# Self-attention phase: output projection, norm and query projection on 13 flat tiles of 128 tokens instead of 16 batches of 100

## The chip, the cores and the metric

The kernel runs on one core of a Trainium2 chip. The metric is the device time of one execution in microseconds (us). Four engines compute: TensorE (PE; its weight loads are a row of their own, PEld), VectorE (DVE), ScalarE (ACT) and GpSimd (POOL). SyncE (SP) only issues transfers. Each engine works through its own list of instructions in order, and they wait for each other on semaphores.

## The reference

A decoder block on x (16 batches of 100 tokens, 512 features): causal self-attention, cross-attention on a context of 361 tokens per batch, and a mixture of experts, each followed by a layer norm. The part that matters here:

```python
x = _layernorm(x + attn(x, w_q, w_k, w_v, w_o))      # causal, 16 heads of 32
q = (x @ Wq + bq).reshape(b, s, 16, 128)             # cross-attention, first step
q = _rmsnorm(q, qn_w)                                # per token and head
k = _rmsnorm(ctx @ Wk + bk, kn_w); v = ctx @ Wv + bv # 4 heads, each shared by 4 of q
out = softmax(q k^T / sqrt(128)) v @ Wo
```

## The kernel before

There are three phases, one behind the other: self-attention (tiles `a_...`), cross-attention (`b_...`), experts (`c_...`). The change is in the first, `self_attention_phase`, and in how the second loads the queries.

The first phase walks over the batches, one body per batch, in a software pipeline written by hand. `over_batches` writes out batches 0 and 1, loops over pairs up to batch 13, and writes out batches 14, 15 and a body 16 that has only the "back" half. Body i does on PE, in this order:

- front half, batch i: scores (L252, 16 small matmuls), the first 3 of 12 matmuls for V;
- back half, batch i-1: four transposes of the normed rows x1 (L266);
- the other 9 matmuls for V;
- back half: the query projection, four products (n = 0 to 3) of 12 matmuls with 512 columns each (`product3`, L65, `a_Wqh`). I call one product with its norm and transposes a **unit**: it gives 100 tokens x 4 heads;
- the transposes of the softmax (L288), which wait for POOL (L540); the transposes of units 0 and 1 (L232); probabilities times V (L300); four matmuls of the next pair's q or k projection (L212); the transposes of units 2 and 3; the other twelve of L212; the output projection (L65, `a_woh`, 12 matmuls), which the residual and norm on DVE follow (L511 to L518).

Products are made from high and low halves (names in h and l), so that each needs three matmuls per 128 rows of the contraction. For a unit, DVE adds the bias (L472) and squares (L479), POOL takes the power -1/2 (L547, L549), DVE scales (L437). After the transposes ACT makes the high half (L336) and DVE the low half (L442) in `a_qo`, two slots, and SP stores it to `q_d` (L196). ACT waits until a slot's last store has landed before it writes the slot again.

At the start the weights w_v, w_o and the four parts of Wq go through `a_stage`, two slots of 1 MB. ACT casts the high half (`split_hi`, L322), DVE subtracts (`split_lo`, L393), and then SP may refill the slot.

The second phase loads 400 KB of queries per group of four heads (`load_q`), two slots, 64 loads.

Of the kernel before, what the change touches and what calls it, by code (L numbers as in the profile page):

```python
# [69 lines left out]
def self_attention_phase(nc, sem, x_nat, xT, w_q, w_k, w_v, w_o, Wq, bq, qn_w, kn_w, causal, ident, x1_d, q_d):  # L70
# [5 lines left out]
    with ExitStack() as ctx:  # L76
# [21 lines left out]
        xs = sb("a_xs", [S, D])  # L98
# [7 lines left out]
        oTh, oTl = sb("a_oTh", [P, DC, S], F32R), sb("a_oTl", [P, DC, S], F32R)  # L106
        x1_s = sb("a_x1", [S, D])
        stat = sb("a_stat", [S, 6])
        mv = sb("a_mv", [S, 2])
        rstd = sb("a_rstd", [S, 1])  # L110
        x1Th, x1Tl = sb("a_x1Th", [P, DC, S], F32R), sb("a_x1Tl", [P, DC, S], F32R)
        qn = sb("a_qn", [S, XKV, XG * XHD])
        junk = sb("a_junk", [S, XG * XHD])
        qss = sb("a_qss", [S, XH])
        qrs = sb("a_qrs", [S, XH])
        qo = sb("a_qo", [P, 2, 2, XG * S], F32R)
# [25 lines left out]
        def over_batches(eng, body):  # L142

            body(0, 0, 0)
            body(1, 1, 0)
            with eng.Fori(1, B // 2 - 1) as pair:
                body(2 * pair, 0, pair)
                body(2 * pair + 1, 1, pair)  # L150
            body(B - 2, 0, B // 2 - 1)
            body(B - 1, 1, B // 2 - 1)
            body(B, 0, B // 2)
# [7 lines left out]
        def _(sp):  # L161
# [9 lines left out]
            sp.dma_start(xs[:], x_nat[0]).then_inc(x_in, 16)  # L171
            sp.dma_start(stage[:, 1], pieces[1][0]).then_inc(w_raw[1], 16)
            sp.dma_start(bq_s[:], bq.partition_broadcast(S)).then_inc(bq_in, 16)
            def body(i, par, pair):
                is_int = isinstance(i, int)
                back, front = not (is_int and i == 0), not (is_int and i == B)
                if par == 0 and has_next(pair):

                    sp.wait_ge(xT_lo, pair + 1)
                    if not back:  # L180
                        sp.wait_ge(qs_done, 2)
                    sp.dma_start(xTr[:], xT[bass.ds(pair + 1, 1)].rearrange("a p c t -> p (a c) t")).then_inc(xT_in, 16)
                if not back:
# [3 lines left out]
                if back:  # L187
                    wait(sp, x1_rdy, i)
                    sp.dma_start(x1_d[bass.ds(i - 1, 1)].rearrange("a t d -> t (a d)"), x1_s[:]).then_inc(x1_out, 16)
                    if front:  # L190
                        wait(sp, ysum, i)
                        sp.dma_start(xs[:], x_nat[bass.ds(i, 1)].rearrange("a t d -> t (a d)")).then_inc(x_in, 16)
                    for n in range(4):
                        wait(sp, qT_lo, 4 * (i - 1) + n + 1)
                        dst = q_d[bass.ds(4 * (i - 1) + n, 1)].rearrange("a p h t -> p (a h) t")
                        sp.dma_start(dst, qo[:, n % 2].bitcast(F32)).then_inc(q_out[n % 2], 16)  # L196
            over_batches(sp, body)
            sp.wait_ge(x1_out, 16 * B)
            for slot in q_out:
                sp.wait_ge(slot, 16 * 2 * B)  # L200

        @block.tensor
        def _(pe):
# [20 lines left out]
            def transpose_q(i, n):  # L224

                pe.wait_ge(q_rdy, 4 * (i - 1) + n + 1)
                if n < 2:
                    pe.wait_ge(q_ev, 4 * (i - 1) + 3 + n)
                else:
                    pe.wait_ge(qT_lo, 4 * (i - 1) + n - 1)  # L230
                for h in range(XG):
                    mm = pe.transpose(bank[4 + n % 2][:, h * S:(h + 1) * S],  # L232
                                      qn[:, n, h * XHD:(h + 1) * XHD], ident_s[0:S, 0:S])
                mm.then_inc(qT_done, 1)

# [4 lines left out]
            def body(i, par, pair):  # L240
                is_int = isinstance(i, int)
                back, front = not (is_int and i == 0), not (is_int and i == B)
# [12 lines left out]
                if front:  # L255

                    pe.wait_ge(xT_lo, pair + 1)
                    if is_int and i == 0:
                        pe.wait_ge(w_lo, 1)
                    product3(pe, bank[7][0:S, :], lambda c: xTh[:, c, cols], lambda c: xTl[:, c, cols],  # L260
                             lambda c: wvh[:, c, :], lambda c: wvl[:, c, :], range(1), last=False)
                if back:

                    wait(pe, x1_rdy, i)
                    for c in range(DC):
                        mm = pe.transpose(bank[6][:, c * S:(c + 1) * S], x1_s[:, c * P:(c + 1) * P], ident_s[0:S, 0:S])  # L266
                    mm.then_inc(x1T_done, 1)
# [5 lines left out]
                if back:  # L273

                    wait(pe, x1T_lo, i)
                    for n in range(4):
# [1538 lines left out]
```

## Time and profile before

| | us |
|---|---|
| median of 3 runs | 1625.73 (1622.57 to 1629.63) |
| the profiled execution | 1628.02, of it the span 1626.2 |
| PE busy in the span | 1482.5 (91%) |
| DVE, ACT, POOL busy | 970.8, 655.5, 639.2 |
| mean granted clock of TensorE | 0.957 of 2.4 GHz |
| first phase | 0 to 529.2 |

Time is counted from the span's start. A timeline row has the start, the duration, engine, line, operation, names with shapes, and a count; in brackets the idle time ahead of it and what ended it. Durations of matmuls overlap, since they are pipelined: the pace is the distance from start to start.

### The profile page before, as it was taken

To read this page: it belongs to the slowest core of one execution; us is meant where nothing else is said; L and a number is where in the kernel's file an instruction comes from. 1 tells how busy PE (TensorE), PEld (TensorE's weight loads), DVE (VectorE), ACT (ScalarE), POOL (GpSimd) and SP (SyncE) were. 2 spreads that over 40 slices of the span, in tenths; PEclk is the share of its full clock that TensorE was granted. 3 is DMA by queue.
4 is the path that set the end of the run, shared out by engine and by line. 5 is a ranking of instruction groups with operands and counts; after the bars stand their busy time and mean duration, and the time that the engine had idled before them with its cause. 6 is when DMAs were issued, how large, how long until landed. Compare 5 with 4: busy or idle time off the path is not lost. (4 is left out here: it accounts for less than half of the span.)

```text
span 1626.2 us, 27742 instructions
## 1 busy us (share of the span) xinstructions
PE 1482.5 (91%) x8494; PEld 1217.7 (75%) x8494; DVE 970.8 (60%) x3587; ACT 655.5 (40%) x1762; POOL 639.2 (39%) x994
## 2 busy tenths in 40 slices
PE   7999999999995689999999999999999998479876
PEld 6778878778764478888888888888888887458754
DVE  3666566666664475556655566555665565744468
ACT  4443343344331254443444444344444444433344
POOL 1334333343342364444443444434344342262173
PEclk8999999999998789999999999999999999579988
DMA  6311212212212441112111111211112110756472
GB/s 204 107 67 62 100 60 78 86 58 81 81 51 86 150 132 42 60 54 64 56 45 59 54 59 39 67 59 54 53 42 68 53 43 21 293 139 167 138 223 81
DMA packets 60957, 139.75 MB, mean 86 GB/s; under 512 B 10182, under 2 KB 21034, under 8 KB 59876
## 3 DMA queue, kind: packets, MB, share of 16 engines
q1 hardware_dynamic: 56296, 123.85, 22.9%
q0 software_dynamic: 4576, 14.95, 3.7%
q8 instruction: 31, 0.51, 0.1%
q14 instruction: 54, 0.44, 0.1%
HBM read 94.31 MB, written 44.46 MB: 85 GB/s over the span
## 5 line engine op out<-in xcount | busy, mean ns | idle before, releaser
L913 ACT ACTIVATE b_probs<-b_probs,b_nmax 100x361 f32<-100x361 f32 x256 | 151.9, 593 | 70.7 <-DVE b_nmax L1011 70.4
L65 PE MATMUL b_bank<-b_kTh,b_q 128*100 128x362 f32 x512 | 174.3, 341 | 3.0 <-DVE b_kTl L993 1.7
L1123 POOL TENSOR_TENSOR b_pcarry<-b_half 128x1 f32<-128x1 f32 x176 | 41.7, 237 | 327.5 <-DVE b_rinv L1017 271.7
L1011 DVE CUSTOM_DVE_ANT_0 b_probs<-b_bank,b_mask 100x361 f32<-100x361 f32 x256 | 135.5, 529 | 56.9 <-issue 46.9
L1148 POOL TENSOR_SCALAR b_probs<-b_probs,b_rinv 100x361 f32<-100x361 f32 x256 | 157.4, 627 | 0.0
L1004 DVE TENSOR_TENSOR b_pTl<-b_bank,b_pTh 121x400 fp32r<-121x400 f32 x192 | 110.0, 573 | 52.6 <-ACT b_pTh L908 51.3
L908 ACT ACTIVATE b_pTh<-b_bank 121x400 fp32r<-121x400 f32 x192 | 96.8, 504 | 102.1 <-PE b_bank L754 99.9
L949 ACT ACTIVATE b_oTh<-b_bank,b_bv 128x400 fp32r<-128x400 f32 x64 | 38.1, 595 | 210.2 <-PE b_bank L65 210.2
L754 PE MATMUL b_bank<-b_ident,b_probs 100*121 100x100 f32 x768 | 110.4, 266 | 5.8 <-POOL b_probs L1148 5.8
L754 PEld LDWEIGHTS b_bank<-b_ident,b_probs 100*121 100x121 f32 x768 | 108.4, 187 | 8.2 <-POOL b_probs L1148 7.3
L65 PE MATMUL b_bank<-b_Woh,b_oTh 128*100 128x512 f32 x256 | 108.0, 422 | 1.4 <-DVE b_oTl L1078 1.4
L1078 DVE SCALAR_TENSOR_TENSOR b_oTl<-b_bank,b_bv,b_oTh 128x400 fp32r<-128x400 f32 x64 | 40.5, 633 | 109.0 <-ACT b_oTh L949 109.0
L65 PE MATMUL a_bank<-a_Wqh,a_x1Th 128*100 128x512 f32 x256 | 101.4, 396 | 2.6 <-DVE a_qn L472 1.4
L65 PEld LDWEIGHTS b_bank<-b_kTh,b_q 128*100 128x100 f32 x512 | 85.6, 167 | 22.0 <-issue 9.2
L65 PE MATMUL a_bank<-a_Wqh,a_x1Tl 128*100 128x512 f32 x256 | 101.7, 397 | 0.0
L65 PE MATMUL a_bank<-a_Wql,a_x1Th 128*100 128x512 f32 x256 | 101.4, 396 | 0.0
L65 PE MATMUL b_bank<-b_Woh,b_oTl 128*100 128x512 f32 x256 | 101.2, 395 | 0.0
L65 PE MATMUL b_bank<-b_Wol,b_oTh 128*100 128x512 f32 x256 | 101.2, 395 | 0.0
L65 PE MATMUL b_bank<-b_Wkh,b_ctxh 128*121 128x512 f32 x192 | 84.0, 437 | 16.2 <-DVE b_Wkl L966 16.2
L357 ACT ACTIVATE a_probs<-a_probs,a_nmax 100x100 f32<-100x100 f32 x256 | 92.8, 366 | 4.4 <-DVE a_nmax L425 4.4
L540 POOL TENSOR_TENSOR a_probs<-a_probs,a_rinv 100x400 f32<-100x400 f32 x64 | 54.6, 853 | 95.2 <-DVE a_rinv L432 95.1
L65 PE MATMUL b_bank<-b_kTl,b_q 128*100 128x362 f32 x256 | 84.8, 331 | 0.0
(241 smaller groups left out, 3981.1 us busy)
## 6 DMA issues: line engine op xcount, KB each, us to landing
q_d<-a_qo SPq DMA_DIRECT2D x64, 400.0 KB, 2.4
b_q<-q_d SPq DMA_DIRECT2D x64, 400.0 KB, 3.1
b_ctxr<-in_ctxT SPq DMA_DIRECT2D x48, 242.0 KB, 4.0
c_Eraw<-in_expert_w SPq DMA_DIRECT2D x16, 512.0 KB, 11.2
y_d<-c_y SPq DMA_DIRECT2D x32, 256.0 KB, 3.6
a_stage<-in_Wq SPq DMA_DIRECT2D x4, 1024.0 KB, 4.8
stage<-in_Wo SPq DMA_DIRECT2D x8, 512.0 KB, 3.7
a_xTr<-in_xT SPq DMA_DIRECT2D x8, 400.0 KB
```

The source lines that it names most:

```text
L65: mm = eng.matmul(out, lhsT=l(c), rhs=r(c), start=first and k == 0, stop=last and k == n - 1)
L357: e = act.activation(probs[:, r, c, :], probs[:, r, c, :], ACT.Exp, scale=-1.0, bias=nmax[:, h:h + 1], accum_out=psums[:, r, c:c + 1])
L540: pool.tensor_tensor(probs[:, r], probs[:, r], rinv[:, r].unsqueeze(2).to_broadcast([S, DC, S]), ALU.mult).then_inc(pn_rdy, 1)
L754: mm = pe.transpose(t_bank[c % 2][0:KT, h * S:(h + 1) * S], probs[:, s % 2, h, c * KT:(c + 1) * KT], ident_s[0:S, 0:S])
L908: act.activation(pTh[:, c, :], t_bank[c % 2][0:KT, 0:XG * S], ACT.Copy).then_inc(pt_hi, 1)
L913: act.activation(p, p, ACT.Exp, scale=-1.0, bias=nmax[:, s % 2, h:h + 1], accum_out=psums[:, s % 2, h:h + 1]).then_inc(e_rdy, 1)
L949: act.activation(oTh[:, kv, :], o_bank[:, 0:XG * S], ACT.Identity, bias=bv_s[:, kv:kv + 1]).then_inc(o_hi, 1)
L1004: dve.tensor_tensor(pTl[:, c, :], t_bank[c % 2][0:KT, 0:XG * S], pTh[:, c, :].bitcast(F32), ALU.subtract).then_inc(pt_lo, 1)
L1011: dve.tensor_tensor_reduce(out=probs[:, s % 2, h, 0:SE], in0=s_bank[h % 2][0:S, 0:SE], in1=mask_s[:], scale=-1.0, scalar=BIG, op0=ALU.add, ...
L1078: dve.scalar_tensor_tensor(out=oTl[:, kv, :], in0=o_bank[:, 0:XG * S], scalar=bv_s[:, kv:kv + 1], in1=oTh[:, kv, :].bitcast(F32), op0=ALU.add,
L1123: pool.tensor_tensor(pcarry[:, k:k + 1], half_s[:, 0:1], half_s[:, 0:1], ALU.add)
L1148: pool.tensor_scalar(p, p, rinv[:, s % 2, h:h + 1], 1.0, ALU.mult, ALU.mult).then_inc(p_rdy, 1)
```

## The change

The 1600 tokens of all batches are taken as one row of tokens and cut into tiles of 128: twelve full ones and one of 64. Output projection, residual, norm, x1 transposes and the units run per tile (52 units in place of 64; unit k is part k % 4 of tile k // 4). The attention output goes into a ring of two tiles (`a_oTh`, `a_oTl`), of which a batch writes 100 columns. Scores, softmax and V stay per batch. All loops are written out. `out_tile` says after which batch a tile is complete: none after batches 0, 4, 9 and 13, and the last after batch 15. `units` says how many units each of the 18 bodies takes. The weights go through the shared `stage` in halves of 512 KB, and w_o no longer has a slot from the start. `q_d` is laid out by tokens, so that one store writes 1024 pieces of 512 bytes, and one load reads 1024 pieces of 400 bytes.

```diff
-        pieces = [(w_v, wvh[:], wvl[:]), (w_o, woh[:], wol[:])]
-        pieces += [(Wq[n], Wqh[:, n], Wql[:, n]) for n in range(4)]
+        pieces = []
+        for w, h, l in [(w_v, wvh[:], wvl[:]), (w_o, woh[:], wol[:])] + [(Wq[n], Wqh[:, n], Wql[:, n]) for n in range(4)]:
+            pieces += [(w[:, c:c + 2], h[:, c:c + 2], l[:, c:c + 2]) for c in range(0, DC, 2)]
+        out_tile = {min((t * P + P - 1) // S, B - 1): t for t in range(NT - 1)}
+        units = [0, 0, 4, 3, 3, 2, 3, 4, 3, 3, 3, 3, 4, 3, 2, 4, 4, 4]
...
+            def store_q(k):
+                t, n = divmod(k, 4)
+                sp.wait_ge(qT_lo, k + 1)
+                sp.dma_start(q_d[n][:, :, :, tokens(t)], qo[:, k % 2, :, :, 0:rows(t)].bitcast(F32)).then_inc(q_out[k % 2], 16)
...
+            def queries(k, start):
+                t, n = divmod(k, 4)
+                pe.wait_ge(x1T_lo, t + 1)
+                if k - 2 >= start:
+                    pe.wait_ge(q_ev, k - 1)
+                else:
+                    wait(pe, qT_lo, k - 1)
...
+            def transpose_q(k, ks):
+                n = rows(k // 4)
+                pe.wait_ge(q_rdy, k + 1)
+                if k + 2 in ks:
+                    pe.wait_ge(q_ev, k + 3)
+                elif k - 2 in ks:
+                    pe.wait_ge(qT_lo, k - 1)
...
+                if i - 1 in out_tile:
+                    transpose_x1(out_tile[i - 1])
+                if i == B:
+                    pe.wait_ge(x1T_lo, NT - 1)
+                    output(NT - 1)
+                if i == B + 1:
+                    transpose_x1(NT - 1)
...
+                for k in ks:
+                    queries(k, ks[0])
...
+                for k in ks[:2]:
+                    transpose_q(k, ks)
...
+                for k in ks[2:]:
+                    transpose_q(k, ks)
...
+                if i in out_tile:
+                    output(out_tile[i])
...
-                src = q_d[bass.ds(n, 1)].rearrange("a p h t -> p (a h) t")
-                sp.dma_start(q_s[:, slot].bitcast(F32), src).then_inc(q_in[slot], 16)
+                src = q_d[n][:, :, :, bass.ds(j * S, S)]
+                sp.dma_start(q_s[:, slot].bitcast(F32).rearrange("p k (h t) -> p k h t", h=XG), src).then_inc(q_in[slot], 16)
...
-    q_d = nc.dram_tensor("q_d", (B * XKV, P, 2, XG * S), F32, kind="Internal").ap()
+    q_d = nc.dram_tensor("q_d", (XKV, P, 2, XG, B * S), F32, kind="Internal").ap()
```

**Place 1: ACT at the start of the program.** Before, the first casts of weights (`a_wvh`, `a_woh`, `a_Wqh`) and the exponentials of batches 0 and 1 (`a_probs`) stand so:

```order
L322 ACTIVATE a_wvh<-a_stage 128x2048
L322 ACTIVATE a_woh<-a_stage 128x2048
L357 ACTIVATE a_probs,a_psums<-a_probs,a_nmax 100x100 x16
L363 ACTIVATE a_v<-a_bank 100x512
L366 ACTIVATE a_pT<-a_bank 100x400 x4
L322 ACTIVATE a_Wqh<-a_stage 128x2048
L375 ACTIVATE a_oTh<-a_bank 128x400
L322 ACTIVATE a_Wqh<-a_stage 128x2048 x2
L350 ACTIVATE a_x1Th<-a_bank 128x400
```

In the changed kernel:

```order
L363 ACTIVATE a_wvh<-stage 128x1024 x2
L363 ACTIVATE a_woh<-stage 128x1024 x2
L405 ACTIVATE a_probs,a_psums<-a_probs,a_nmax 100x100 x16
L411 ACTIVATE a_v<-a_bank 100x512
L414 ACTIVATE a_pT<-a_bank 100x400 x4
L363 ACTIVATE a_Wqh<-stage 128x1024 x2
L424 ACTIVATE a_oTh<-a_bank 128x4x100
L363 ACTIVATE a_Wqh<-stage 128x1024 x4
L405 ACTIVATE a_probs,a_psums<-a_probs,a_nmax 100x100 x16
L363 ACTIVATE a_Wqh<-stage 128x1024 x2
```

Each cast is now two, and each waits for a slot of its own. The cast of x1 is gone from batch 1, since no tile is complete after batch 0.

**Place 2: PE behind the units of one batch.** Before, every batch has eight transposes of `a_qn` (units 0 and 1) and eight more (units 2 and 3):

```order
L288 MATMUL a_bank<-a_ident,a_probs 100x100 x16
L232 MATMUL a_bank<-a_ident,a_qn 128x100 x8
L300 MATMUL a_bank<-a_pT,a_v 32x100 x16
L212 MATMUL a_bank<-a_xTr,a_wq 128x200 x4
L232 MATMUL a_bank<-a_ident,a_qn 128x100 x8
L212 MATMUL a_bank<-a_xTr,a_wq 128x200 x12
```

In batch 3 of the changed kernel, one of eight with three units:

```order
L335 MATMUL a_bank<-a_ident,a_probs 100x100 x16
L280 MATMUL a_bank<-a_ident,a_qn 128x128 x8
L346 MATMUL a_bank<-a_pT,a_v 32x100 x16
L238 MATMUL a_bank<-a_xTr,a_wq 128x200 x4
L280 MATMUL a_bank<-a_ident,a_qn 128x128 x4
L238 MATMUL a_bank<-a_xTr,a_wq 128x200 x12
```

The third unit is the last, so the second unit's transposes come one product after its own, where two products lay between before.

**Place 3: ACT at the end of the phase**, from the last batch's output (`a_oTh`) on. Before:

```order
L375 ACTIVATE a_oTh<-a_bank 128x400
L336 ACTIVATE a_qo<-a_bank,a_qkw 128x400 x2
L350 ACTIVATE a_x1Th<-a_bank 128x400
L336 ACTIVATE a_qo<-a_bank,a_qkw 128x400 x4
L76 UNCONDITIONAL_BRANCH
```

In the changed kernel:

```order
L424 ACTIVATE a_oTh<-a_bank 128x4x64
L378 ACTIVATE a_qo<-a_bank,a_qkw 128x512 x2
L384 ACTIVATE a_x1Th<-a_bank 128x512
L378 ACTIVATE a_qo<-a_bank,a_qkw 128x512 x4
L384 ACTIVATE a_x1Th<-a_bank 128x4x64
L378 ACTIVATE a_qo<-a_bank,a_qkw 128x4x64 x4
L76 UNCONDITIONAL_BRANCH
```

There are two rounds of x1 cast and four units behind the last batch, where there was one. The cast of the last tile's x1 stands behind the casts of the units before it.

## Rows read from the trace of the kernel before

**Rows 1.** The page: busy share of PE in 40 slices, tenths

```profile
PE   7999999999995689999999999999999998479876
```

**Rows 2.** Busy time by stage of the first phase; behind the engines: granted clock, DMA share, GB/s

```profile
0.00:79.40 79.40, 66.19 (x404) 54.64 (x405) 39.88 (x149) 35.51 (x94) 18.17 (x26) 0.94 0.48 157
79.40:496.15 416.75, 409.07 (x2793) 326.90 (x2792) 264.11 (x1291) 165.74 (x620) 150.54 (x208) 1.00 0.20 73
496.15:529.20 33.05, 16.46 (x68) 11.68 (x68) 14.61 (x51) 2.90 (x6) 6.72 (x10) 0.75 0.21 81
```

**Rows 3.** Timeline of PE in one steady batch (199.8 to 229.9)

```profile
203.16 0.56 PE L266 MATMUL a_bank<-a_ident,a_x 100*128 100x100 f32 x4 [0.24 <-DVE a_x L518]
...
205.60 0.39 PE L65 MATMUL a_bank<-a_Wqh,a_x1Th 128*100 128x512 f32 x1
...
216.71 1.54 PE L288 MATMUL a_bank<-a_ident,a_probs 100*100 100x100 f32 x16
218.08 0.85 PE L232 MATMUL a_bank<-a_ident,a_qn 100*128 100x100 f32 x8
218.86 1.99 PE L300 MATMUL a_bank<-a_pT,a_v 100*32 100x100 f32 x32
...
226.88 0.54 PE L65 MATMUL a_bank<-a_woh,a_oTh 128*100 128x512 f32 x1
...
229.85 2.26 PE L252 MATMUL a_bank<-a_kTs,a_qTs 32*100 32x100 f32 x32
```

**Rows 4.** The same batch on POOL, DVE, ACT and SP

```profile
210.34 0.85 POOL L540 TENSOR_TENSOR a_probs<-a_probs,a_rinv 100x400 f32<-100x400 f32 x1 [0.60 <-DVE a_rinv L432]
...
218.60 0.68 DVE L437 TENSOR_TENSOR a_qn<-a_qn,a_qrs 100x512 f32<-100x512 f32 x1
220.46 0.69 DVE L437 TENSOR_TENSOR a_qn<-a_qn,a_qrs 100x512 f32<-100x512 f32 x1 [1.18 <-POOL a_qrs L549]
...
224.28 0.59 ACT L336 ACTIVATE a_qo<-a_bank,a_qkw 128x400 fp32r<-128x400 f32 x1 [2.88 <-DMA q_d<-a_qo]
```

**Rows 5.** Start: first split (timeline of DVE); a half-size split (groups by line)

```profile
21.70 2.29 DVE L393 TENSOR_TENSOR a_wvl<-a_stage,a_wvh 128x2048 fp32r<-128x2048 f32 x1 [6.92 <-ACT a_wvh L322]
...
L966 DVE TENSOR_TENSOR b_Wkl<-stage,b_Wkh 128x1024 fp32r<-128x1024 f32 x2 | 2.5, 1226 | 6.0 <-ACT b_Wkh L894 6.0
```

**Rows 6.** Transfers: name, queue, count, KB each, median us to landing; SP's timeline

```profile
q_d<-a_qo SPq DMA_DIRECT2D x64, 400.0 KB, 2.4
b_q<-q_d SPq DMA_DIRECT2D x64, 400.0 KB, 3.1
stage<-in_Wo SPq DMA_DIRECT2D x8, 512.0 KB, 3.7
a_wk<-in_w_k SPq DMA_DIRECT2D x4, 256.0 KB, 4.8
...
1.65 2.69 SPq L166 DMA_DIRECT2D a_wk<-in_w_k  x4
```

**Rows 7.** Timeline of the phase's end: PE, ACT and SP

```profile
499.92 0.93 PE L266 MATMUL a_bank<-a_ident,a_x 100*128 100x100 f32 x4 [3.77 <-DVE a_x L518]
502.04 0.75 PE L65 MATMUL a_bank<-a_Wqh,a_x1Th 128*100 128x512 f32 x1 [1.20 <-DVE a_x1Tl L454]
...
514.98 0.51 PE L232 MATMUL a_bank<-a_ident,a_qn 100*128 100x100 f32 x4
...
525.02 0.59 ACT L336 ACTIVATE a_qo<-a_bank,a_qkw 128x400 fp32r<-128x400 f32 x1 [1.68 <-DMA q_d<-a_qo]
...
529.16 0.34 SPq L673 DMA_DIRECT2D b_ctxr<-in_ctxT  x1
```

**Rows 8.** Timeline of PE in the third phase: matmuls with 128-wide weights

```profile
1579.64 0.39 PE L65 MATMUL c_bank<-c_Phl,c_cTl 128*128 128x512 f32 x1
1579.87 0.61 PE L65 MATMUL c_bank<-c_Phl,c_cTh 128*128 128x512 f32 x2
```

**Rows 9.** The second phase's wait for its query slot: SP's waits, 560 to 1300

```profile
SPq L678 <- PE b_bank L65: 372.9, 44, 14.8
```

More of the change, by code:

```diff
@@ L67, in product3, with self_attention_phase @@
     return mm
-def self_attention_phase(nc, sem, x_nat, xT, w_q, w_k, w_v, w_o, Wq, bq, qn_w, kn_w, causal, ident, x1_d, q_d):
+def self_attention_phase(nc, sem, stage, x_nat, xT, w_q, w_k, w_v, w_o, Wq, bq, qn_w, kn_w, causal, ident, x1_d, q_d):
     with ExitStack() as ctx:
@@ L186, in body @@
                         sp.dma_start(stage[:, n % 2], pieces[n][0]).then_inc(w_raw[n % 2], 16)
[L187 to L198, printed above, removed]
+                if i - 1 in out_tile:
+                    store_x1(out_tile[i - 1])
+                for k in new_units(i):
+                    store_q(k)
+            store_x1(NT - 2)
+            store_x1(NT - 1)
+            for i in (B, B + 1):
+                for k in new_units(i):
+                    store_q(k)
+            sp.wait_ge(x1_out, 16 * NT)
             for slot in q_out:
-                sp.wait_ge(slot, 16 * 2 * B)
+                sp.wait_ge(slot, 16 * 2 * NT)
         @block.tensor
@@ L238, in _ @@
             pe.wait_ge(consts, 48)
-            def body(i, par, pair):
-                is_int = isinstance(i, int)
-                back, front = not (is_int and i == 0), not (is_int and i == B)
+            for i in range(B + 2):
+                pair, par = divmod(i, 2)
+                front, ks = i < B, new_units(i)
                 if front:
@@ L343, in _ @@
             split_hi(1)
-            def body(i, par, pair):
-                is_int = isinstance(i, int)
-                back, front = not (is_int and i == 0), not (is_int and i == B)
-                if back:
-                    wait(act, x1T_done, i)
-                    act.activation(x1Th[:].rearrange("p c t -> p (c t)"), bank[6][:, 0:DC * S],
-                                   ACT.Copy).then_inc(x1T_hi, 1)
+            for i in range(B + 2):
+                pair, par = divmod(i, 2)
+                front, ks = i < B, new_units(i)
+                if i - 1 in out_tile:
+                    x1_transposed(out_tile[i - 1])
+                if i == B + 1:
+                    x1_transposed(NT - 1)
                 if front:
@@ L446, in body, with query_squares @@
-            def body(i, par, pair):
-                is_int = isinstance(i, int)
-                back, front = not (is_int and i == 0), not (is_int and i == B)
+            def query_squares(k):
+                t, n = divmod(k, 4)
+                m = rows(t)
+                dve.wait_ge(qx_done, k + 1)
+                dve.tensor_tensor(qn[0:m, n], bank[4 + k % 2][0:m, :], bq_s[0:m, n * D:(n + 1) * D], ALU.add).then_inc(q_ev, 1)
+                wait(dve, q_ss, k)
+                dve.wait_ge(q_ev, k + 1)
+                for h in range(XG):
+                    q = qn[0:m, n, h * XHD:(h + 1) * XHD]
+                    e = dve.tensor_tensor_reduce(out=junk[0:m, h * XHD:(h + 1) * XHD], in0=q, in1=q, scale=1.0,
+                                                 scalar=0.0, op0=ALU.mult, op1=ALU.add,
+                                                 accum_out=qss[0:m, XG * n + h:XG * n + h + 1])
+                e.then_inc(q_ss, 1)
@@ L449, in body @@
+            for i in range(B + 2):
+                pair, par = divmod(i, 2)
+                front, ks = i < B, new_units(i)
                 if front:
@@ L495, in body @@
-                if back:
-                    queries_lo(i, 2)
-                    queries_lo(i, 3)
+                    for a, at, n in batch_in_ring(i):
+                        e = dve.tensor_tensor(oTl[:, :, at:at + n], bank[7][:, 0:DC * S].rearrange("p (c t) -> p c t", c=DC)[:, :, a:a + n],
+                                              oTh[:, :, at:at + n].bitcast(F32), ALU.subtract)
+                    e.then_inc(oT_lo, 1)
+                for k in ks[2:]:
+                    queries_lo(k)
```

360 lines of the change are left out of this document (183 added, 177 removed).

## The prediction

> **What bounds the kernel now.** I first read the page. PE is busy nine tenths or more in all slices but the first, those around 500 us and the last seven; the dip at 500 us is the seam between the first and the second phase [rows 1]. Only the first phase is rebuilt, so I cut it by the windows view into start, steady part and end [rows 2]. In the steady part PE is busy for 409.1 of 416.75 us at the full 2.4 GHz, DVE for 264, ACT for 166. There PE's own work is the time, and a matmul taken away is time gained. In the start (79.4 us, granted clock 0.94) and the end (33.05 us, PE busy for 16.5, clock 0.75) chains over several engines set the time, and there work on PE costs more than its own length.
>
> Next, one steady batch on PE. The four units take 216.71 - 205.60 = 11.11, so 2.78 for the twelve matmuls of a unit; eight transposes take 218.86 - 218.08 = 0.78, so 0.39 for a unit; the output projection 229.85 - 226.88 = 2.97; the x1 transposes about 0.6 with their wait of 0.24 [rows 3].
>
> **The steady part, from the scores of batch 2 to the output of batch 15.**
> - Units: 14 batches x 4 = 56 before; from batch 2 to 15 the list has 44. 12 x (2.78 + 0.39) = -38.0.
> - Output projections: 14 before, tiles 1 to 11 now: 3 x 2.97 = -8.9. The x1 transposes: 14 before, 11 now: -1.8.
> - Wider tiles: the weights are 128 columns in place of 100. In the third phase such matmuls start 0.23 apart [rows 8], as the 0.23 of the units here: nothing for the products. Transposes have 28% more columns. 55 groups of four at 0.39; I give each 0.02, between nothing and 28% (+6): +1.3.
> - The waits behind the units. With four units, POOL has the last softmax tile at 211.2 and PE wants it from 216.71 [rows 3, 4]. Three units bring PE there 2.8 earlier, two 5.6; both batches with two units (5 and 14) follow one without a finished tile, so DVE has no norm ahead of the masks and starts some 3 earlier. The softmax stays hidden. The unit's own chain does not. DVE scales the last unit but one from 218.60 to 219.28, which is 2.6 behind the end of the last product, and the last one to 221.15, 4.4 behind it [rows 3, 4]. With four units PE asks for neither before the products with V. With three it wants the last but one after the softmax transposes (1.37) and one unit's transposes (0.39): it waits 2.6 - 1.8 = 0.8. There are eight such batches: +6.4. With two units the waits are 1.2 and 1.5: two batches, +5.4. Batch 14 has no next projection between V and output, and output needs the split on ACT and DVE: +1.3. Batch 15 still waits for its slot: +1.0. Against that goes what stood there before: 416.75 - 409.07 = 7.7 idle, less 14 x 0.24 = 4.3. Sum +9.8. The lower bound is 0.
>
> Sum: -38.0 - 8.9 - 1.8 + 1.3 + 9.8 = **-37.6**.
>
> **The stores.** ACT writes a slot of `a_qo` again only when its last store has landed; now that is 2.4 behind the issue [rows 6], and ACT waits for it in each batch [rows 4]. A store becomes 512 KB in 1024 pieces of 512 B. The nearest rows are the loads of wk, pieces of 512 B, too: 512 pieces in 0.67 of SP (2.69 for four), and 4.8 to land behind others [rows 6]. I take 3.7, an estimate: some 0.7 more on SP, whose issue of such a store should come to twice wk's 0.67, and 0.6 more to move 112 KB more in smaller pieces. Bounds: 2.4 (no change) and 5.6 (moving takes three times as long). In the steady part there is room: ACT's third cast starts at 224.28 and DVE is next wanted for the residual at 229.9 [rows 3, 4], so 1.3 costs nothing, and 5.6 next to nothing. At the end it stands on the path, below.
>
> **The start.** w_v and w_o were both in their slots from the beginning. Now the halves of w_o are loaded only when the halves of w_v have been split. The first split of 2.29 began at 21.70, so w_o was done at 26.3 and the masks of batch 0 began behind it [rows 5]. Now the first half is cast some 0.9 earlier and split in 1.23, free at 22.0; 3.7 to land [rows 6] gives 25.7, and the second, freed at 23.2, lands at 26.9; cast 1.0, split 1.2: 29.2. So batch 0 is 3 later. It has no output projection (-3). Batch 1 has no tile and no units: PE has only scores and V to cover the softmax. Moreover the casts of the third Wq part stand ahead of its exponentials on ACT (place 1), and those wait for slots freed by the splits of the second, by my count at 49 and 50. They land at 52.7 and 53.9, so the exponentials run from 55 to 61, then come the two casts of the fourth part, V's copy and the softmax copies to 65, products with V to 66, the projection and its clock loss to 71.5, output to 74.5. I take 75.0 for the scores of batch 2 in place of 79.4: **-4.4**. If half a megabyte takes 4.8 to land, as wk did, twice on this chain, it is +2.2.
>
> **The end.** Before, from the last output (496.15) to the second phase's first issue (529.16): 33.0. Now two tiles are left there, one behind the other (place 3):
> - to the first product 502.04 - 496.15 = 5.9 [rows 7], plus 1.3 since the last batch's stores delay DVE: 7.2;
> - the last tile's output 2.8, and 1.8 for the clock: 48 matmuls took 514.98 - 502.04 = 12.9 where they take 11.1 at full clock: 4.6;
> - units 44 to 47: 11.1;
> - then ACT casts the four units before the last x1 (place 3). The last cast began 525.02 - 514.98 = 10.0 behind the products, waiting for a store; plus 1.3, the cast, x1's cast and split: 12.5;
> - units 48 to 51, PE having stood still at half clock: 12.9;
> - the last four stores as before, 529.16 - 514.98 = 14.2, less 0.7 for 64 columns: 13.5.
>
> 61.8 in place of 33.0: **+28.8**. With stores of 2.4 it is 5 less, with 5.6 it is 8 more.
>
> **The second phase.** 64 loads in pieces of 400 B. SP waits 372.9 us for free slots in 44 loads [rows 9]: a slot is refilled while a whole group runs from the other, against 3.1 to land [rows 6]. Twice that stays hidden. The one at the phase's beginning stands among the first weights: +0.8, between 0 and 3. The Trainium skill (DMA: Bandwidth & Descriptors, Specifications) asks for at least 512 B to run at line rate and says that below it the engine reads, modifies and writes. That speaks against the 400 B loads and the last tile's stores of 256 B. By it two landings more on the end's path would double their moving time, some 3 us, and the sum would be -9 in place of -12; no row here shows such pieces.
>
> **Sum.** -37.6 - 4.4 + 28.8 + 0.8 = -12.4. The profiled execution took 1628.02, so 1615.6; it lay 2.3 above the median of 1625.73, so I give **1613.3**. Of the 48.7 us of PE work that goes (12 units, 3 outputs, 3 groups of x1 transposes) three quarters come back, as waits and as a longer end.
>
> **The rivals.**
> - *The waiting is smaller* (0.14). If the third and second units' chains find PE later than I count (6.4 + 5.4 fall away) and stores stay at 2.4, it is -12.4 - 9 = -21: 1604. For it speaks that DVE, with fewer units, runs less behind; against it that the 2.6 and 4.4 are a chain of fixed lengths.
> - *Stores and refills are slow* (0.20). Stores land in 5.6 (+8), refills in 4.8 (+2.2): -2: 1623. For it the 4.8 of wk; against it that wk stood behind other transfers.
> - *Slower* (0.12): small pieces are much slower than in wk's case. The third cast starts 224.28 - 216.71 = 7.6 behind the last product with a landing of 2.4 [rows 3, 4], so 5.2 plus the landing; DVE is wanted 13.2 behind that product. Past about 7 us of landing DVE comes late for the residual in each of 13 tiles, while the end pays four times. At 8 us: 13 x 0.7 + 4 x 4.3 = +26, so +14: 1640. The gain is gone from 6.8 us on. Against it: wk's 512 pieces ran at 4.8 in a full queue.
> - *As counted* (0.54): 1613, its own range 1607 to 1619.
>
> **How the numbers follow.** A measurement of this kernel tells about 0.5%, 8.1 us, from no change. Faster than 1617.6: the first rival, and all but a little of my own case: 0.66. Within: the second rival and the rest: 0.22. Slower: 0.12. The range, 1602 to 1627, holds both faster cases and the second rival, and leaves out the slow one.
>
> **What would show it.** In the profile after: scores of batch 2 at 75, the first phase's end at about 517 in place of 529.2; PE's idle time ahead of the query transposes 0.8 in eight batches; a median landing of the `q_d` stores of 3.7; two gaps of PE of 5 us or more at the end, with the clock at half behind each; no wait of PE for `b_q`. It is wrong if the stores land past 6, if the exponentials of batch 1 start well before or behind 55, or if unrolled code makes PE wait for instructions, which the written-out batches 14 and 15 of before do not show.

## The result and the profile after

The changed kernel is **slower**: 1643.63 us median of 4 runs (1640.24 to 1647.17) against 1627.68 of the kernel before beside it; ratio 1.0091, 95% interval 1.0071 to 1.0111. Run once more with eight runs it gave 1639.72, ratio 1.0065 (1.0039 to 1.0091). So it loses 0.7 to 0.9%, some 11 to 16 us, where I had forecast a gain of 12.4. One of the seven executions of e7_whole below took 7281 us and is left out of all its numbers.

The page of the changed kernel, the same slices as [rows 1], with the granted clock (PEclk, in tenths of 2.4 GHz):

```profile
PE   5799999999876579999999999999999999469976
...
PEclk8799999999888799999999999999999999579988
```

PE is below nine tenths in two slices at the beginning and in five around 500 us, where there were one and three; the first of the five (from 410 us) lies in the steady part. Cut at the same places as [rows 2] (scores of batch 2, end of the last full tile's output, first issue of the second phase), columns as there:

```profile
0.00:81.17 81.17, 54.74 (x324) 47.33 (x324) 28.13 (x105) 33.78 (x95) 10.04 (x16) 0.81 0.42 132
81.17:473.95 392.78, 374.61 (x2553) 314.73 (x2552) 227.30 (x1146) 162.70 (x609) 129.25 (x178) 0.98 0.26 78
473.95:537.91 63.96, 35.59 (x149) 23.76 (x148) 29.05 (x102) 6.89 (x12) 13.40 (x20) 0.77 0.29 78
```

| stage | before | forecast of the difference | measured difference |
|---|---|---|---|
| start | 79.40 | -4.4 | +1.8 |
| steady part | 416.75 | -37.6 | -24.0 |
| end | 33.0 | +28.8 | +30.9 |
| second and third phase | 1097.0 | +0.8 | +3.5 |
| sum | 1626.2 | -12.4 | +12.2 |

**The steady part** can be taken apart. PE is idle for 392.78 - 374.61 = 18.2; the forecast's waits came to 7.7 + 9.8 = 17.5. But PE is *busy* for 374.61 where the forecast makes it 361.7 (409.07 less 47.4). The missing 12.9 lies in PE's own work. Part of it is seen in batch 14 (PE's timeline; the bracket is the idle time ahead and who ended it):

```profile
420.15 2.26 PE L307 MATMUL a_bank<-a_kTs,a_qTs 32*100 32x100 f32 x32 [0.59 <-ACT a_qTs L367]
...
424.20 0.63 PE L65 MATMUL a_bank<-a_wvh,a_xTl 128*100 128x512 f32 x1
...
434.99 0.66 PE L280 MATMUL a_bank<-a_ident,a_qn 128*128 128x128 f32 x4 [1.09 <-DVE a_qn L502]
436.86 1.12 PE L280 MATMUL a_bank<-a_ident,a_qn 128*128 128x128 f32 x4 [1.21 <-DVE a_qn L502]
437.90 3.56 PE L346 MATMUL a_bank<-a_pT,a_v 100*32 100x100 f32 x32
```

The second products with V take 3.56, where they took 1.99 [rows 3]. The windows view of the same batch shows why; the third number from the end is the granted clock:

```profile
420.00:424.00 4.00, 3.85 (x37) 3.30 (x38) 3.12 (x27) 2.21 (x9) 0.00 (x0) 0.85 0.43 122
424.00:428.00 4.00, 4.00 (x14) 2.86 (x14) 1.35 (x14) 4.00 (x24) 2.32 (x3) 0.72 0.00 0
...
436.00:440.00 4.00, 3.14 (x26) 2.81 (x28) 2.10 (x3) 1.06 (x2) 0.08 (x1) 0.56 0.33 94
440.00:444.00 4.00, 2.80 (x17) 2.25 (x15) 0.57 (x1) 0.50 (x1) 0.00 (x0) 0.50 0.58 169
```

PE runs at 1.2 GHz twice inside one batch: once behind a wait of 0.59 ahead of the scores, once behind the waits of 1.09 and 1.21 ahead of the query transposes. In [rows 2] the steady part stood at 1.00 on the mean. That mean hides one fall. In the last batch of the steady part of the kernel before, the clock falls too, behind a wait of 2.63 (PE's timeline, and the windows view):

```profile
472.12 0.93 PE L266 MATMUL a_bank<-a_ident,a_x 100*128 100x100 f32 x4 [2.63 <-DVE a_x L518]
...
471.00:475.00 4.00, 2.88 (x10) 2.17 (x11) 3.33 (x29) 1.92 (x10) 0.48 (x1) 0.59 0.33 92
```

The first wait in batch 14 of the changed kernel follows batch 13, one of the batches that have no output projection: before, an output projection of 3 us covered the copies of the next queries and keys out of the banks by ACT and DVE in every batch. The Trainium skill (TensorE: Matmul & The Clock Gate, A second HAM failure mode: psum-queue depth-cycling) describes a clock that swings because PE idles briefly between groups of matmuls. The trace agrees that the falls stand behind brief idle times; other executions have the same idle times without the fall (after_again, below).

**The start.** ACT's casts and PE's softmax transposes:

```profile
25.75 1.06 ACT L363 ACTIVATE a_woh<-stage 128x1024 fp32r<-128x1024 f32 x1 [4.35 <-DMA stage<-in_w_o]
29.87 1.06 ACT L363 ACTIVATE a_woh<-stage 128x1024 fp32r<-128x1024 f32 x1 [3.07 <-DMA stage<-in_w_o]
...
55.62 1.06 ACT L363 ACTIVATE a_Wqh<-stage 128x1024 fp32r<-128x1024 f32 x1 [5.61 <-DMA stage<-in_Wq]
57.74 1.06 ACT L363 ACTIVATE a_Wqh<-stage 128x1024 fp32r<-128x1024 f32 x1 [1.07 <-DMA stage<-in_Wq]
```

```profile
35.71 0.91 PE L335 MATMUL a_bank<-a_ident,a_probs 100*100 100x100 f32 x4 [8.17 <-POOL a_probs L619]
...
61.87 1.93 PE L335 MATMUL a_bank<-a_ident,a_probs 100*100 100x100 f32 x8 [6.06 <-POOL a_probs L619]
...
67.49 3.53 PE L346 MATMUL a_bank<-a_pT,a_v 100*32 100x100 f32 x32 [0.80 <-ACT a_pT L414]
```

The first half of w_o comes when forecast (25.7); the second is cast at 29.87 in place of 26.9. The exponentials of batch 1 begin at 58.7 in place of 55, and what follows runs at half clock.

**The end**, on ACT and on PE:

```profile
475.12 0.69 ACT L378 ACTIVATE a_qo<-a_bank,a_qkw 128x512 fp32r<-128x512 f32 x1 [5.52 <-DMA q_d<-a_qo]
...
508.27 0.69 ACT L378 ACTIVATE a_qo<-a_bank,a_qkw 128x512 fp32r<-128x512 f32 x1 [6.42 <-DMA q_d<-a_qo]
...
532.34 0.47 ACT L378 ACTIVATE a_qo<-a_bank,a_qkw 128x256 fp32r<-128x256 f32 x1 [5.86 <-DMA q_d<-a_qo]
```

```profile
481.06 1.11 PE L254 MATMUL a_bank<-a_ident,a_x 128*128 128x128 f32 x4 [6.97 <-DVE a_x L531]
...
511.90 0.69 PE L65 MATMUL a_bank<-a_Wqh,a_x1Th 128*64 128x512 f32 x1 [4.64 <-DVE a_x1Tl L516]
```

Three times ACT is idle for 5.5 to 6.4 us until a store has landed, and PE has gaps behind them, in the places that the forecast named. Transfers of the changed kernel:

```profile
b_q<-q_d SPq DMA_DIRECT2D x64, 400.0 KB, 3.8
q_d<-a_qo SPq DMA_DIRECT2D x48, 512.0 KB, 3.6
```

The landing is 3.6 (2.4 before [rows 6], forecast 3.7).

### The profile page after: what moved, and what is told of

Its sections match the earlier page's. It is cut to its first block and busy times, and to the rows that moved or that the text cites. A ratio compares the mean times of both kernels' runs of the same rounds, so it can differ in the third digit from the quotient of the medians.

```text
span 1638.4 us, 26309 instructions
## 1 busy us (share of the span) xinstructions
PE 1455.5 (89%) x8254; PEld 1210.5 (74%) x8254; DVE 935.7 (57%) x3449; ACT 654.1 (40%) x1759; POOL 617.3 (38%) x964
## 5 line engine op out<-in xcount | busy, mean ns | idle before, releaser
L65 PE MATMUL a_bank<-a_Wqh,a_x1Th 128*128 128x512 f32 (+1 forms) x208 | 82.9, 398 | 4.6 <-DVE a_x1Tl L516 4.6
L65 PE MATMUL a_bank<-a_Wql,a_x1Th 128*128 128x512 f32 (+1 forms) x208 | 82.6, 397 | 0.0
L65 PE MATMUL a_bank<-a_Wqh,a_x1Tl 128*128 128x512 f32 (+1 forms) x208 | 82.6, 397 | 0.0
```

What stands on the lines that cost most here:

```text
L65: mm = eng.matmul(out, lhsT=l(c), rhs=r(c), start=first and k == 0, stop=last and k == n - 1)
```

## The experiments

Medians with the ratio to the kernel before beside them, and the profiled execution of each, cut at the scores of batch 2, the start of the last full tile's output projection, and the second phase's first issue (so its "end" is about 3 longer than that of the table above):

| kernel | median, ratio (95%) | start | steady | end | rest |
|---|---|---|---|---|---|
| before | 1627.7 | 79.4 | 413.8 | 36.0 | 1097.0 |
| changed | 1643.6, 1.0091 (1.0071 to 1.0111) | 81.2 | 389.8 | 66.9 | 1100.5 |
| e1_layout | 1653.4, 1.0155 (1.0134 to 1.0176) | 78.7 | 430.3 | 41.3 | 1103.2 |
| e2_unroll | 1626.8, 0.9998 (0.9987 to 1.0010) | 79.3 | 410.8 | 34.8 | 1097.6 |
| e3_load4 | 1633.3, 1.0029 (1.0017 to 1.0041) | 68.7 | 395.6 | 66.7 | 1100.5 |
| e4_store4 | 1627.2, 0.9990 (0.9974 to 1.0007) | 81.0 | 392.1 | 58.4 | 1097.4 |
| e5_both | 1620.7, 0.9954 (0.9937 to 0.9971) | 68.6 | 385.6 | 58.1 | 1101.4 |
| e6_units | 1635.3, 1.0038 (1.0026 to 1.0050) | 79.2 | 386.1 | 67.8 | 1098.2 |
| e7_whole | 1633.1, 1.0035 (1.0010 to 1.0059) | 80.0 | 385.5 | 65.1 | 1095.9 |
| after_again | 1639.7, 1.0065 (1.0039 to 1.0091) | 82.1 | 387.4 | 66.3 | 1097.4 |
| e8_ks | 1601.0, 0.9829 (0.9811 to 0.9847) | 70.7 | 368.2 | 57.9 | 1102.7 |
| e9_tail | 1604.9, 0.9848 (0.9827 to 0.9869) | 70.5 | 392.3 | 43.9 | 1100.5 |
| e10_all | 1583.4, 0.9731 (0.9701 to 0.9762) | 67.6 | 368.2 | 43.9 | 1098.9 |
| e11_layout_slots | 1628.1, 1.0001 (0.9989 to 1.0012) | 79.4 | 410.0 | 36.7 | 1098.7 |

The rest of two executions of the changed kernel differs by 3.1, so one such number tells no single microsecond.

**e1_layout: the kernel before with the new layout of the queries alone.**

```
-dst = q_d[bass.ds(4 * (i - 1) + n, 1)].rearrange("a p h t -> p (a h) t")
+dst = q_d[n][:, :, :, bass.ds((i - 1) * S, S)]
-q_d = nc.dram_tensor("q_d", (B * XKV, P, 2, XG * S), F32, kind="Internal").ap()
+q_d = nc.dram_tensor("q_d", (XKV, P, 2, XG, B * S), F32, kind="Internal").ap()
```

> The kernel before, with nothing changed but where the queries lie in q_d: stores by batch and loads by batch in pieces of 400 B, both sides. My theory is that the new layout costs little by itself: stores land in 3.0 to 3.7 in place of 2.4, which is 1 us at each of the two stores on the phase's end, and the second phase loses the 3.4 us that it lost in the changed kernel; so 4 to 6 us over the kernel before, 1632 to 1634. The rival is that small pieces are the main cause of the loss (with 400 B on both sides, the stores land past 5, and the end and every batch pay for it): then 10 us or more, 1638 and above.

It lost 25 us: my theory's number failed. The rival's size came true (10 us or more), though its condition did not: the stores land in 4.2, not past 5. In the profiled execution 16.5 are in the steady part, 5.3 at the end, 6.2 in the rest. Its transfers, and its waits from 110 to 480 (us in total, times, longest):

```profile
q_d<-a_qo SPq DMA_DIRECT2D x64, 400.0 KB, 4.2
b_q<-q_d SPq DMA_DIRECT2D x64, 400.0 KB, 3.8
```

```profile
ACT a_qo L337 <- DMA q_d<-a_qo: 64.9, 22, 4.7
...
DVE a_qo L443 <- ACT a_qo L337: 56.8, 22, 4.1
...
PE a_bank L267 <- DVE a_x L519: 6.8, 6, 1.5
```

In the same stretch of the kernel before ACT waited 41.7 and DVE 32.8. So 1.8 us more of landing make DVE 2 us later in each of the twelve batches, and DVE has not that room: PE waits for the norm and for the keys, and behind such waits the clock falls in four of the batches. In PE's timeline of batch 3 the matmuls behind the scores start about 0.43 apart, where they start 0.23 apart at full clock:

```profile
110.92 2.79 PE L253 MATMUL a_bank<-a_kTs,a_qTs 32*100 32x100 f32 x32 [1.46 <-DVE a_kTn L399]
114.19 0.63 PE L65 MATMUL a_bank<-a_wvl,a_xTh 128*100 128x512 f32 x1
114.61 0.63 PE L65 MATMUL a_bank<-a_wvh,a_xTl 128*100 128x512 f32 x1
```

**e11_layout_slots: the same, with four store slots** (the other two in the weight stage, which is free by then).

```
-wait(act, q_out[n % 2], 16 * (2 * (i - 1) + n // 2))
+wait(act, q_out[n], 16 * (i - 1))
```

> The kernel before with its queries in pieces of 400 B, as in the first experiment, and with four store slots in place of two. Theory: the 25 us of the first experiment come through the landing of 4.2 us in place of 2.4, for which ACT waits twice in each batch, and through DVE behind it; the slots take ACT out of it, so that about 5 us of the second phase's loads and some 2 of the last stores remain: 1630 to 1637. Rival: small pieces slow the batches in another way (SP, which issues longer, or the other transfers): 1645 or more.

All 25 us are back, more than expected (1630 to 1637), although the stores land later still:

```profile
q_d<-a_qo SPq DMA_DIRECT2D x32, 400.0 KB, 5.2
q_d<-a_stage SPq DMA_DIRECT2D x32, 400.0 KB, 6.6
```

So in this kernel small pieces cost nothing measurable (ratio 0.9989 to 1.0012) once nobody waits for the landing. The rest is 1098.7 here and 1103.2 in e1_layout with the same loads, so the 6.2 that e1_layout lost there can't all be the loads.

**e7_whole: the changed kernel with whole blocks** (the loads then read other tokens' queries).

```
-sp.dma_start(q_d[n][:, :, :, tokens(t)], qo[:, k % 2, :, :, 0:rows(t)].bitcast(F32))...
+dst = q_d.rearrange("(a p x) -> a p x", p=P, x=2 * XG * P)[k]
+sp.dma_start(dst, qo[:, k % 2].bitcast(F32).rearrange("p a h t -> p (a h t)"))...
```

> The changed kernel, but each store of queries writes one whole block of 512 KB and each load reads one whole block of 400 KB, in the pieces of 4096 and 3200 B that the blocks have in each partition. The loads of the second phase then read other tokens' queries than the kernel should (the output is not the reference's; the work is the same). It shows what the small pieces cost in the changed kernel by themselves. Theory: stores land in 2.6 to 2.8 in place of 3.6, 1 us at each of three stores on the end's path, and the second phase gets back its 3.4: 6 to 8 us off, 1636 to 1638. Rival, after the kernel before lost 25 us by pieces of 400 B alone: the small pieces are the main cause of the loss, and 14 us or more come back: 1630 or less.

```profile
q_d<-a_qo SPq DMA_DIRECT2D x52, 512.0 KB, 2.6
b_q<-q_d SPq DMA_DIRECT2D x64, 400.0 KB, 3.1
```

Against the changed kernel timed next to it (after_again) it gains 1.0065 - 1.0035 = 0.3%, 5 us; the intervals overlap, so that it may be nothing or some 10. Landings go from 3.6 to 2.6 and from 3.8 to 3.1. The rival (14 us or more) is out: the pieces are a small part of the changed kernel's loss. That this is because DVE has room with three units in most batches fits e1_layout, but was not tried by itself.

**e2_unroll: the kernel before with its loop over batches written out.**

```
-with eng.Fori(1, B // 2 - 1) as pair:
+for i in range(B + 1):
+    body(i, i % 2, i // 2)
```

> The kernel before with the first phase's loop over the batches written out, nothing else. Theory: no difference (within 2 us of the kernel before), since no engine waited for instructions in the changed kernel that I could see. Rival: the written-out code costs time by itself, in the first phase or behind it (the second phase of the changed kernel was 3.4 us longer): then 3 us or more here too, and the second phase shows it although its code and its data are those of before.

No difference; the rival is out. The profiled execution has a steady part 3.0 shorter all the same, and that tells of the kernel before. In batch 14 of its profiled execution ACT waited longer for a store to land, DVE made the last low half of the queries at 468.4, where e2_unroll does it at 466.7, the norm came later, and the x1 transposes waited 2.63 in place of 0.69, with the fall of the clock behind them. So one late landing cost the kernel before some 3 us too, and against an execution without it the steady part gained 21 and not 24.

**e3_load4: four 512 KB slots for the weights.**

```
+raw = [stage[:, 0], stage[:, 1]] + [qo[:, s].bitcast(F32).rearrange("p a h t -> p a (h t)") for s in (0, 1)]
-for n in range(2, len(pieces)):
-    sp.wait_ge(w_lo, n - 1)
+for n in range(4, len(pieces)):
+    sp.wait_ge(w_lo, n - 3)
```

> The changed kernel with four 512 KB load slots (the two of stage and the two of a_qo, which is free until batch 2) for the halves of w_v, w_o and Wq, so that w_o is on its way from the start again. Theory: the start lost its forecast gain by the refills that pass through two small slots and by PE's clock behind them; with four slots the masks of batch 0 begin at 27 to 29 in place of 32, the exponentials of batch 1 at 53 to 56 in place of 58.7, and the scores of batch 2 at 74 to 77 in place of 81.2: 4 to 7 us off the changed kernel, 1637 to 1640. Rival: the start is set by the four Wq parts (4 MB to be loaded and split), not by the slots: then 2 us or less.

The start is 12.5 shorter, more than expected. PE's softmax transposes of batches 0 and 1 come 7.0 and 10.5 earlier:

```profile
28.73 0.55 PE L336 MATMUL a_bank<-a_ident,a_probs 100*100 100x100 f32 x4 [1.11 <-POOL a_probs L620]
...
51.38 0.55 PE L336 MATMUL a_bank<-a_ident,a_probs 100*100 100x100 f32 x4 [2.49 <-POOL a_probs L620]
```

**e4_store4: four slots for the query stores.**

```
-wait(act, q_out[k % 2], 16 * (k // 2))
+wait(act, q_out[k % 4], 16 * (k // 4))
```

> The changed kernel with four slots for the query stores (two in stage, which is free by batch 2), so that ACT no longer waits for a landing. Theory: in the steady part nothing (0 to 2 us), at the end the waits of 5.5, 6.4 and 5.9 us of ACT for q_d go, of which 12 to 16 us are on the path: 1628 to 1632, the end 48 to 52 in place of 64. Rival: the end is set by PE, its clock and the chain of the last units, and the landing is hidden behind them: less than 5 us.

The median, 1627.2, lies just under the expected range (1628 to 1632), but the end is only 8.5 shorter, where 12 to 16 were expected. ACT's wait goes over to PE, whose transposes now come last:

```profile
504.32 0.69 ACT L381 ACTIVATE stage<-a_bank,a_qkw 128x512 fp32r<-128x512 f32 x1 [3.89 <-PE a_bank L283]
```

What else the medians differ by lies in the rest (3.1 in these two executions) and in the clock of batches 5 and 14; I can't divide it.

**e5_both: four slots for both.** Its diff is that of the two above.

> The changed kernel with four slots for both, weights at the start and query stores after it (the four of the two experiments before, the same memory in turn). Theory: start and end are separate losses, so their gains add: -10.3 of the four load slots and -16.4 of the four store slots on 1643.6 give 1617, 11 us under the kernel before. Rival: they overlap, or a batch's clock takes part of it back: 1622 or more.

1620.7, between the theory's 1617 and the rival's 1622: the stages show both gains whole (68.6 and 58.1), the rest is 1101.4. It is faster than the kernel before by 0.5%.

**e6_units: no batch with two units.**

```
-units = [0, 0, 4, 3, 3, 2, 3, 4, 3, 3, 3, 3, 4, 3, 2, 4, 4, 4]
+units = [0, 0, 3, 3, 3, 3, 3, 4, 3, 3, 3, 3, 3, 3, 3, 4, 4, 4]
```

> The changed kernel with the units spread so that no batch has two: 3, 3, 3, 3 in batches 2 to 5 for 4, 3, 3, 2, and 3, 3, 3 in batches 12 to 14 for 4, 3, 2. Nothing else differs; as many units in all. Theory: in the two-unit batches PE stands still twice for more than 1 us within 4 us, and behind it the granted clock is at half for some 4 to 9 us in batch 5, in batch 14 or in both, another one in each run, which is also why the changed kernel's runs lie 7 us apart. Without them: two waits of 2.3 go, four of 0.7 come, and 4 to 9 us of half clock go: 6 to 11 us off, 1633 to 1638, and the runs lie closer. Rival: the spread and the clock have another cause: within 2 us of the changed kernel.

4.4 off against the changed kernel timed next to it, and the runs lie closer (1631 to 1638 against 1633 to 1645). That is less than the theory's 6, and the intervals overlap. The clock still falls, now in batches 10 and 14, where the only wait ahead is that for the scores, behind a batch without output. So the waits of two-unit batches are not the only place where it falls. What they cost through the clock this run can't tell, since executions that have them differ among themselves (next experiment).

**after_again.**

> The changed kernel itself once more, for a second profile and more runs beside the others. Theory: 1640 to 1647 as before; if the profiled run is one of the slower ones, batch 5 is longer than 26.5 us and has a stretch at half clock, as batch 5 of the two experiments with four slots had. Rival: the slower ones lose their time elsewhere, in the second or third phase.

The profiled execution was one of the quick ones (1635.0), so the question of the slower ones was not answered by it. Beside the first it is 5.2 shorter in its span: 3.1 in the rest and 2.4 in batch 14, whose second stretch at half clock is shorter, less a start that is 0.9 longer. Batch 5 took 26.0 in both, but 30.4 in the executions of e3_load4 and e4_store4, with half clock in it.

Batch 14 settles what the fall of the clock costs by itself. PE has the same instructions in it, in the same order, in the changed kernel, in its second run, in e5_both and in e7_whole, and the same three waits (1.09, 1.21 and 1.20). The windows view of that batch in after, after_again and e5_both:

```profile
420.15:447.49 27.34, 23.83 (x137) 18.85 (x137) 11.18 (x64) 10.64 (x41) 6.22 (x8) 0.75 0.19 55
420.99:445.94 24.95, 21.44 (x136) 16.99 (x136) 11.19 (x64) 10.65 (x41) 6.22 (x8) 0.86 0.20 60
408.77:430.67 21.90, 18.39 (x137) 14.74 (x137) 11.14 (x64) 10.65 (x41) 6.22 (x8) 1.00 0.17 50
```

PE is idle for 3.51 in each; the batch takes 27.3 at a mean clock of 0.75, 24.9 at 0.86 and 21.9 at 1.00 (21.9 in e7_whole too). So the clock alone costs up to 5.4 us here, and nothing in some executions. Batch 5 goes from 26.0 to 30.4 in the same way. Together that is up to 10 us, the size of the spread between executions of the changed kernel (1632.8 to 1647.2). Why it falls in one execution and not in another, none of these runs shows.

**e8_ks: e5_both with the units of e6_units, and transposes moved.**

```
+def ahead(i):
+    return 2 if i >= B or len(new_units(i)) > 3 else 1
-for k in ks[:2]:
+for k in ks[:ahead(i)]:
...
+if front and i not in out_tile:
+    for k in ks[ahead(i):]:
+        transpose_q(k, ks)
```

> The kernel with four slots for both, the spread units, and two moves in the order of each batch: of three units only the first is transposed ahead of the products with V, the other two behind them; and in the batches without an output projection (4, 9, 13) these two stand behind the next projection. Theory: twelve waits of 0.7 ahead of the transposes go (-8.5), the waits of 0.6 ahead of the scores of batches 5, 10 and 14 go (-2), and with them the stretches at half clock, which stood right behind these waits (-2 to -6): 1604 to 1610. Rival: the scaling on DVE is as late for the transposes behind V, or the casts on ACT now come late for something else: 1616 or more.

1601.0, 20 us off, more than expected. The steady part to the end of output 11 (windows) and batch 5 on PE (timeline):

```profile
70.72:441.80 371.08, 366.47 (x2553) 310.90 (x2552) 227.51 (x1148) 163.24 (x611) 129.28 (x178) 1.00 0.28 82
```

```profile
165.15 0.60 PE L288 MATMUL a_bank<-a_ident,a_qn 128*128 128x128 f32 x4
165.68 1.99 PE L354 MATMUL a_bank<-a_pT,a_v 100*32 100x100 f32 x32
...
169.06 1.04 PE L288 MATMUL a_bank<-a_ident,a_qn 128*128 128x128 f32 x8
```

No bracket ahead of a transpose in batch 5, a clock of 1.00, and as many matmuls as in the changed kernel, 2553, busy for 366.47 in place of 374.61. Waits of 0.8 and 0.9 ahead of transposes stay in batches 14 and 15. The spread units and the two moves came together, and were not told apart.

**e9_tail: e5_both with another end.**

```
+output(NT - 1)
+transpose_x1(NT - 2)
+for group in ("Q44", "Q45", "X", "Q46", "Q47", "T44", "T45", "Q48", "Q49", "T46", "T47", "Q50", "Q51",
+              "T48", "T49", "T50", "T51"):
```

(Q: products of a unit, X: x1 transposes of tile 12, T: transposes of a unit.)

> The kernel with four slots for both, and the phase's end rearranged: the output of tile 12 right behind that of tile 11 in a bank of its own, its x1 transposes behind two units' products, and the last eight units' products, transposes and casts interleaved over six banks. Same work. Theory: the end is a chain of two tiles that need not follow one another; PE is left with one gap ahead of unit 44, and the end (from the last output to the second phase's first issue) falls from about 59 to 43 to 47: 12 to 16 us off, 1605 to 1609. Rival: the second phase's start or the clock takes it back: less than 6 us.

The end went from 58.1 to 43.9.

**e10_all: e8_ks and e9_tail together.**

> Both of the changes before together. Theory: they touch different stretches and add up: 1590 to 1597, 2% under the kernel before. Rival: one of them hid the other's wait: 1603 or more.

1583.4, **2.7% faster than the kernel before** and better than the expected 1590 to 1597. Its stages:

```profile
0.00:67.62 67.62, 51.55 (x325) 44.65 (x325) 27.63 (x105) 33.57 (x95) 10.01 (x16) 0.87 0.49 158
67.62:438.75 371.13, 366.58 (x2554) 311.10 (x2554) 227.48 (x1148) 163.16 (x611) 129.28 (x178) 1.00 0.28 82
438.75:479.72 40.97, 30.26 (x149) 20.66 (x147) 27.15 (x100) 5.30 (x10) 13.07 (x20) 0.92 0.45 121
```

## Why the prediction was wrong

The miss in the profiled execution is 24.6 us: 13.6 in the steady part, 6.2 in the start, 2.7 in the rest, 2.1 in the end. The 13.6 are 0.7 of idle time and 12.9 of PE's busy time: 4.8 through the wider tiles, 5.4 through the clock, and 2.7 of longer matmuls around waits at full clock.

- **Units, output projections and x1 transposes (-48.7): right in mechanism.** With most of the new waits and all of the clock loss gone (e8_ks), PE's busy time is 366.47 against 409.07: -42.6.
- **Wider tiles (+1.3): mis-sized.** -42.6 for -48.7 leaves +6.1, the upper bound that I had given. "I give each 0.02, between nothing and 28%" took a value near the low end without a row for it. A batch with four units and a tile takes 30.7 in place of 30.1; most of it are the transposes. In batch 7 the first eight take 240.63 - 239.66 = 0.97 in place of 0.78, the next eight 0.87 in place of 0.69:

```profile
238.28 1.54 PE L335 MATMUL a_bank<-a_ident,a_probs 100*100 100x100 f32 x16
239.66 1.04 PE L280 MATMUL a_bank<-a_ident,a_qn 128*128 128x128 f32 x8
240.63 2.00 PE L346 MATMUL a_bank<-a_pT,a_v 100*32 100x100 f32 x32
```

  The products of four units take 11.20 there in place of 11.11, so "nothing for the products" was nearly right. That is 4.8 more than counted. It may be 1.3 more still: the 409.07 hold a stretch at half clock, and e2_unroll, with the same work of PE at full clock, is busy for 407.73.
- **The waits behind the units (+9.8): right as waits, wrong as a price.** PE's idle time is 18.2 for 17.5, but two misses nearly cancel in that. The waits ahead of the transposes were 0.65 to 1.08 in the batches with three units (0.8 forecast) and 1.1 and 1.2 in those with two (1.2 and 1.5), together 1.2 less than forecast; waits ahead of scores, 2.8 in all, were not forecast. The step that failed is that a wait costs its own length. The same number of matmuls is busy for 374.61 - 366.47 = 8.1 longer than in e8_ks. Of that 5.4 is the clock in batch 14, as the three executions above show. The other 2.7 lies in batches at full clock. Batch 3 has the same work in both kernels, here first in the changed one, then in e8_ks:

```profile
111.87:140.25 28.38, 27.43 (x189) 23.11 (x188) 16.56 (x81) 12.66 (x45) 9.98 (x14) 1.00 0.31 95
98.19:125.65 27.46, 27.19 (x190) 23.12 (x189) 16.48 (x81) 12.66 (x45) 9.99 (x14) 1.00 0.26 77
```

  A wait of 0.68 more makes it 0.92 longer, since PE is busy 0.24 longer besides. I had counted half clock at the end, but in the steady part not at all. No row that I had picked showed it there; the trace of before did, in its last batch (0.59 from 471 to 475), under a mean of 1.00.
- **Batches without an output projection: not seen.** I counted three output projections as gained and did not ask what they had covered. The waits ahead of the scores of batches 5, 10 and 14 (0.6 to 0.8) are new and gone in e8_ks, which puts transposes where the projection was, and in e6_units and in batch 14 the clock falls behind them.
- **The start (-4.4, measured +1.8): the landing of refills mis-sized.** "3.7 to land" held for the first half of w_o; the second, which SP had issued by 23.2, was cast 6.7 later. `a_bq` can't have held it up, for it had landed at 12.26 + 7.6 = 19.9, before either half was issued; what did stays open. From there the lateness runs on: the masks of batch 0 begin at 32.1 in place of 29.2, SP can refill for the third part of Wq at 51.6 in place of 49, its halves are cast at 55.6 and 57.7, the exponentials of batch 1 begin at 58.7 in place of 55, and with the half clock behind them the scores of batch 2 at 81.2 in place of 75.0. Exponentials of batch 1 well behind 55 were one of the signs that the forecast had named against itself, and the only one that came. The slots were the cause, as e3_load4 shows with -12.5: the rival "stores and refills slow" had the right place but +2.2 for it.
- **The end (+28.8, measured +30.9): right.** Place, gaps and half clock as forecast. That it needn't be so long (e9_tail: 43.9 in place of 66.9, with the store slots) was outside the prediction.
- **The stores (3.7, measured 3.6): right in size, not in its parts.** SP issues such a store in 0.54, where it took 0.33 before; the 0.7 more that I gave SP were 0.2, and the moving took the difference. **"In the steady part there is room": nearly right for the changed kernel** (e4_store4 shows no gain there; only the wait of 0.83 ahead of the scores of batch 13, behind a batch of four units, goes with its slots), but e1_layout shows that the reason given was wrong: with four units in a batch, 4.2 cost 16.5 us, where I had put the point at which DVE comes late at about 7. My slow rival was a false picture; its 1640 came true by other causes, and so by luck.
- **The second phase (+0.8, 0 to 3; measured +3.5): small.** Over the eleven executions with loads in pieces of 400 B the rest is 1097.4 to 1103.2, 1099.9 on the mean; with whole blocks 1095.9, 1097.0 and 1097.6. So 2 to 3 us are possible, but one execution varies by more, and e11_layout_slots, with the same loads, loses nothing over ten runs. By the rule quoted ahead (the Trainium skill, DMA: Bandwidth & Descriptors, Specifications) the sum would have been -9; the traces agree that pieces below 512 B are dearer (1.8 us of 400 KB's landing, e1_layout), but pieces of 512 B are dearer than blocks too (3.6 against 2.6 for 512 KB, e7_whole), and what costs time is the waiting and not the moving.
- **Slips in the sums.** 55 groups at 0.02 are 1.1 and not 1.3. The first rival takes away 6.4 + 5.4 of waits and 5 of stores, 17 us and not 9, so that its time is 1597 and not 1604, below the stated range. Neither would have changed the direction.

## What to carry to other kernels

Where PE's work is the time, a wait put behind shorter work can cost more than its length: here 10.5 us of new idle time came with 8.1 us of longer matmuls, 5.4 of them at half clock in one batch. Look for orders that leave no wait (the order of a few transposes and a list of units gave 20 us here). Ask of each removed instruction what it covered, and of each transfer how many slots stand behind it before asking how fast it is: 25 us that small pieces had cost vanished with two more slots. Flat tiles push work to the end; there the last two tiles should run side by side.

## What the runs showed of the hardware

PE's clock fell to half behind idle times as short as 0.59 us ahead of the scores, and not in each execution: batch 14 of the changed kernel, with the same instructions of PE and the same 3.51 us of idle time, took 27.3, 24.9 and 21.9 us at mean clocks of 0.75, 0.86 and 1.00, and batch 5 took 26.0 at full clock and 30.4 with half clock in it. Stores of 400 KB in 400-byte pieces land in 4.2 us where blocks land in 2.4, and in 5.2 to 6.6 when four may be under way, with no loss of time. Eight transposes with 128 columns took 0.97 us where eight with 100 took 0.78.
